# Attention scores as one float32 matmul for each of two heads, on the two halves of the array's rows

## What is computed

```python
t = tokens * rsqrt(mean(tokens * tokens, -1) + eps) * rms_w
gates = sigmoid(t @ w_gates)
q, k, v = (einsum('bnd,hde->bhne', t, w) for w in (wq, wk, wv))
score = where(causal_mask, -max, einsum('bhie,bhje->bhij', q, k) * scale)
attn = softmax(score, axis=-1)
out = einsum('bhij,bhje->bhie', attn, v) * gates
pred_values = einsum('bhne,hed->bnd', out, wo)
x = layernorm(x + pred_values)
x = layernorm(x + moe(x))      # 16 experts, top 2, and a shared expert
```

## Time and profile before

| | |
|---|---|
| median of 3 runs (lowest, highest) | 684.72 us (682.33, 686.58) |
| profiled execution, first to last instruction | 723.0 us |
| TensorE matmuls busy | 627.0 us, 87% |
| VectorE busy | 485.0 us, 67% |
| ScalarE busy | 417.0 us, 58% |
| GpSimd busy | 116.4 us, 16% |
| start, until the first scores | 0 to 32.5 us |
| attention, four head pairs | 32.5 to about 510 us |
| experts and last norm | about 510 to 723 us |
| mean granted TensorE clock | 0.944 of full speed |

### The profile page before, as it was taken

One profiled execution on the slowest core, in us unless ns is written; L12 is line 12 of the kernel. 1 busy time (PEld: TensorE's weight loads), 2 busy tenths in 40 slices (PEclk: granted clock), 3 DMA queues, 4 the chain that ended last, 5 costly groups with the idle time before them and its releaser, 6 DMA issues.

```text
span 723.0 us, 14787 instructions
## 1 busy us (share of the span) xinstructions
PE 627.0 (87%) x5300; PEld 511.7 (71%) x5300; DVE 485.0 (67%) x1556; ACT 417.0 (58%) x909; POOL 116.4 (16%) x229
## 2 busy tenths in 40 slices
PE   4899999999999999999999999998766079999930
PEld 2688888778888868888886888887623047888830
DVE  4788776698776778876768887767771033665636
ACT  4876566786655687665668766565330012655636
POOL 2000000000000000000000000000327600677630
PEclk9999999999999999999999999999599579999975
DMA  6600000130000040000007920003821100222233
GB/s 152 140 2 1 2 1 3 44 75 1 3 1 1 2 105 14 1 2 2 1 2 166 127 2 2 1 2 124 227 16 52 51 23 11 74 79 78 64 98 105
DMA packets 56393, 33.57 MB, mean 46 GB/s; under 512 B 23809, under 2 KB 49665, under 8 KB 56321
## 3 DMA queue, kind: packets, MB, share of 16 engines
q1 hardware_dynamic: 53760, 27.37, 18.8%
q0 software_dynamic: 2560, 5.26, 2.2%
HBM read 14.75 MB, written 9.48 MB: 34 GB/s over the span
## 4 chain that ended last, share of the span: by engine, by line
PE 74%; DVE 12%; another core or an unknown queue 5%; ACT 3%; issue 2%; DMA 2%; SPq 1%; POOL 0%; DVEq 0%; ACTq 0%; POOLq 0%
PE ps_t L966 18%; PE ps_o L1079 18%; PE ps_s L1048 11%; PE ps_s L1050 9%; PE ps_s L1198 5%; PE ps_o L1089 4%; PE ps_o L1186 3%; DVE k_l L671 3%; DVE q_hl L671 2%; PE ps_s L1122 2%; PE ps_t L1133 1%; PE ps_s L974 1%; ACT k_h L500 1%; DMA act_s<-y_rows 1%
## 5 line engine op out<-in xcount | busy, mean ns | idle before, releaser
L966 PE MATMUL ps_t<-ident,probs 128*128 128x128 f32 x1104 | 173.4, 275 | 11.6 <-ACT probs L512 11.5
L966 PEld LDWEIGHTS ps_t<-ident,probs 128*128 128x128 f32 x1104 | 134.9, 141 | 48.5 <-issue 11.4
L543 ACT ACTIVATE probs<-probs,nmax 128x128 f32<-128x128 f32 (+15 forms) x128 | 153.6, 1200 | 21.1 <-DVE nmax L766 12.4
L775 DVE COPY probsT<-ps_t 128x512 f32<-128x512 f32 (+3 forms) x160 | 91.3, 570 | 101.4 <-PE ps_t L966 100.4
L554 ACT ACTIVATE probsT<-ps_t 128x512 f32<-128x512 f32 (+3 forms) x160 | 89.7, 561 | 98.5 <-PE ps_t L966 97.1
L1048 PE MATMUL ps_s<-k_h,q_hl 128*128 128x512 f32 (+3 forms) x320 | 142.3, 448 | 0.4 <-DMA k_l<-k_l 0.4
L1079 PE MATMUL ps_o<-probsT,v_sb 128*64 128x128 f32 x2176 | 140.0, 277 | 1.3 <-DVE x_acc L790 1.2
L1079 PEld LDWEIGHTS ps_o<-probsT,v_sb 128*64 128x64 f32 x2176 | 116.8, 137 | 19.6 <-issue 14.6
L761 DVE TENSOR_SCALAR_CACHE_REDUCE probs<-ps_s 128x512 f32<-128x512 f32 x192 | 128.4, 686 | 0.7
L1050 PE MATMUL ps_s<-k_l,q_hl 128*128 128x512 f32 (+3 forms) x320 | 117.0, 366 | 0.0
L429 POOL TENSOR_TENSOR rden<-rsum,gate 128x2 f32<-128x2 f32 x64 | 12.6, 197 | 403.9 <-ACT probs L543 392.6
(11 more groups left out here) (144 smaller groups left out, 738.8 us busy)
## 6 DMA issues: line engine op xcount, KB each, us to landing
k_h<-k_h SPq DMA_DIRECT2D x32, 128.0 KB, 2.4
k_l<-k_l SPq DMA_DIRECT2D x32, 128.0 KB, 2.3
w_all<-in_L_ffn_W SPq DMA_DIRECT2D x2, 2048.0 KB, 12.6
xg<-x_sorted SPq DMA_DIRECT2D x48, 64.5 KB
x_sorted<-zeros SPq DMA_DIRECT2D x12, 256.0 KB, 9.5
act_s<-y_rows SPq DMA_DIRECT2D x8, 256.0 KB, 5.4
x_acc<-in_L_attn_tokens SPq DMA_DIRECT2D x4, 256.0 KB, 3.8
out<-x_acc SPq DMA_DIRECT2D x4, 256.0 KB, 2.3
```

The lines of the kernel that those rows point to most:

```text
L543: nc.scalar.activation(probs[s % 2][h][:, 0:w], probs[s % 2][h][:, 0:w], ACT.Exp, bias=nmax[:, row], scale=-1.0, accum_out=rsum[:, row]).t ...
L775: nc.vector.tensor_copy(probsT[s % 2][h][:, c * BT:c * BT + w // P, :].rearrange("p n i -> p (n i)"), ps_t[1][:, 0:w]).then_inc(moved1, 1)
L966: return nc.tensor.transpose(dst, src, ident[:, :])
```

## The change

Scores are made of plain float32. The projected K and Q of a head pair stay as they come out of the projection, head 0 on rows 0 to 63 and head 1 on rows 64 to 127, in one tensor each (`k_t`, `q_t`). A score group of a head is one float32 matmul over its own 64 rows. The two heads of a chunk are queued one behind the other, each into its own bank. ScalarE copies a projection in one operation of 128 rows; VectorE's subtraction and the transfers between the halves are gone. A bank of a projection is free after ScalarE's copy (`high`), so `freed` counts score groups alone, numbered by `score_of`. The order of units changes: scores are listed chunk by chunk with both heads, and the places of scores and turns are rounded to pairs; `ACT_LAG` has two new values; the chunk minima have a second buffer. A tensor `early_w_all` keeps the room that the removed tensors had.

```diff
     PLACE = {"scores": -0.15, "turn": 1.0, "times_v": 0.77, "times_wo": 0.6, "project": 0.0}
-    ACT_LAG = {"scores": 0.1, "turn": -0.3, "times_v": -0.15, "project": -0.3}
+    ACT_LAG = {"scores": 0.0, "turn": -0.2, "times_v": -0.15, "project": -0.3}
     DVE_LAG = {"turn": -0.2, "times_v": -0.4, "times_wo": 0.2}
...
-                stages.append([("scores", s, h, c, w) for h in range(2) for c, w in chunks[s]])
+                stages.append([("scores", s, h, c, w) for c, w in chunks[s] for h in range(2)])
...
-                    place = s + (i + PLACE.get(x[0], 0.5)) / len(units) + lag.get(x[0], 0.0)
+                    i2 = i // 2 * 2 if x[0] in ("scores", "turn") else i
+                    place = s + (i2 + PLACE.get(x[0], 0.5)) / len(units) + lag.get(x[0], 0.0)
...
+    score_of = [numbered(units, ("scores",)) for units in PE_UNITS]
...
-        q_hl = [sb(f"q_hl{h}", [P, N], f32r, attn) for h in range(2)]
-        k_h = [sb(f"k_h{h}", [P, N], f32r, attn) for h in range(2)]
-        k_l = [sb(f"k_l{h}", [P, N], f32r, attn) for h in range(2)]
+        q_t = sb("q_t", [P, N], f32, attn)
+        k_t = sb("k_t", [P, N], f32, attn)
+        sb("early_w_all", [P, 4 * N], f32, attn)
...
-        cmin = sb("cmin", [P, 2, NC], f32, attn)
+        cmin = sb("cmin", [P, 2, 2, NC], f32, attn)
...
-            def k_across(unit, highs, frees):
-                c = unit[3]
-                cols = slice(c * BANK, (c + 1) * BANK)
-                for k_part, part_ready, count in ((k_h, high, highs + 1), (k_l, freed, frees + 1)):
-                    sp.wait_ge(part_ready, count)
-                    for h in range(2):
-                        rows, other = slice(h * DH, (h + 1) * DH), slice((1 - h) * DH, (2 - h) * DH)
-                        sp.dma_start(k_part[h][other, cols].bitcast(f32),
-                                     k_part[h][rows, cols].bitcast(f32)).then_inc(k_twice, 16)
-
-            for x in START:
-                if x[1] == K:
-                    k_across(x, start_high_of[x], start_fill_of[x] + ONE)
-            for p in range(PAIRS - 1):
-                for x in PE_UNITS[0]:
-                    if x[:2] == ("project", K):
-                        k_across(x, p * KQ_FILLS + (KQ_FILLS + high_of[x]),
-                                 p * FREED + (KQ_FILLS + fill_of[x] + ONE))
...
-            sp.wait_ge(freed, ONE + KQ_FILLS + (PAIRS - 1) * FREED + GROUPS)
+            sp.wait_ge(freed, ONE + PAIRS * GROUPS)
...
-                    for h in range(2):
-                        rows = slice(h * DH, (h + 1) * DH)
-                        ins = nc.scalar.activation((k_h, q_hl)[w][h][rows, c * BANK:(c + 1) * BANK],
-                                                   ps_s[n % RING][rows, :], ACT.Copy)
-                    ins.then_inc(high, 1)
+                    nc.scalar.activation((k_t, q_t)[w][:, c * BANK:(c + 1) * BANK],
+                                         ps_s[n % RING][:, :], ACT.Copy).then_inc(high, 1)
...
-                        act.wait_ge(freed, p * FREED + (KQ_FILLS + n + 1 + ONE))
+                        act.wait_ge(freed, p * GROUPS + (n + 1 + ONE))
...
-            def project(unit, n, highs):
-
-                _, w, _, c, _ = unit
-                if w != V:
-                    dve.wait_ge(high, highs + 1)
-                    cols = slice(c * BANK, (c + 1) * BANK)
-                    for h in range(2):
-                        rows = slice(h * DH, (h + 1) * DH)
-                        free = slice((1 - h) * DH, (2 - h) * DH)
-                        low = (k_l[h][rows, cols], q_hl[h][free, cols])[w]
-                        ins = nc.vector.tensor_tensor(low, ps_s[n % RING][rows, :],
-                                                      (k_h, q_hl)[w][h][rows, cols].bitcast(f32), ALU.subtract)
-                    ins.then_inc(freed, 1)
...
-                if i >= 2:
-                    for w in (K, Q):
-                        x = ("project", w, 0, i - 2, 0)
-                        project(x, start_fill_of[x], start_high_of[x])
...
-                    least = cmin[:, h, c:c + 1] if (s, h) in long_rows else nmax[:, row]
+                    least = cmin[:, s % 2, h, c:c + 1] if (s, h) in long_rows else nmax[:, row]
...
-                        dve.wait_ge(freed, p * FREED + (KQ_FILLS + n + 1 + ONE))
-                        nc.vector.tensor_reduce(nmax[:, row], cmin[:, h, 0:c + 1], X, ALU.min).then_inc(row_max, 1)
+                        dve.wait_ge(freed, p * GROUPS + (score_of[("scores", s, h, c, w)] + 1 + ONE))
+                        nc.vector.tensor_reduce(nmax[:, row], cmin[:, s % 2, h, 0:c + 1], X, ALU.min).then_inc(row_max, 1)
...
-                    pe.wait_ge(freed, ONE + n - RING + 1)
+                    pe.wait_ge(high, n - RING + 1)
...
+                filled = {n: x for x, n in fill_of.items()}
+
                 def free_bank(n):
 
                     if n < RING:
                         pe.wait_ge(v_ready, p * NC + (n + 1))
+                        return
+                    held = filled[n - RING]
+                    if held[0] == "scores":
+                        pe.wait_ge(freed, p * GROUPS + (ONE + score_of[held] + 1))
+                    elif held[1] == V:
+                        pe.wait_ge(v_ready, (p + 1) * NC + (NC - held[3]))
                     else:
-                        pe.wait_ge(freed, p * FREED + (ONE + KQ_FILLS + n - RING + 1))
+                        pe.wait_ge(high, (p + 1) * KQ_FILLS + (high_of[held] + 1))
 
                 def scores(s, h, c, w, n):
                     t = ORDER[s]
-                    if s == 0 and h == 0:
-
-                        pe.wait_ge(freed, p * FREED + (ONE + KQ_FILLS))
-
-                        pe.wait_ge(k_twice, p * (64 * NC) + 64 * NC)
+                    if s == 0 and h == 0 and c == 0:
+
+                        pe.wait_ge(high, (p + 1) * KQ_FILLS)
                     free_bank(n)
-                    q = q_hl[h][:, t * P:(t + 1) * P]
-                    nc.tensor.matmul(ps_s[n % RING][:, 0:w], q, k_h[h][:, c * BANK:c * BANK + w],
-                                     start=True, stop=False)
-                    nc.tensor.matmul(ps_s[n % RING][:, 0:w], q, k_l[h][:, c * BANK:c * BANK + w],
-                                     start=False, stop=True).then_inc(fill, 1)
+                    rows = slice(h * DH, (h + 1) * DH)
+                    nc.tensor.matmul(ps_s[n % RING][:, 0:w], q_t[rows, t * P:(t + 1) * P], k_t[rows, c * BANK:c * BANK + w],
+                                     start=True, stop=True).then_inc(fill, 1)
```

More of the change, by code:

```diff
@@ L55, in attention_moe_layer @@
     KQ_FILLS = PROJECTIONS - NC
-    FREED = FILLS - NC
     RING = 4
@@ L126, in attention_moe_layer @@
     start_fill_of = numbered(START, ("project",))
+    score_of = [numbered(units, ("scores",)) for units in PE_UNITS]
     high_of = {x: n for n, x in enumerate(x for x in PE_UNITS[0] if x[0] == "project" and x[1] != V)}
-    start_high_of = {x: n for n, x in enumerate(x for x in START if x[1] != V)}
     def started(*unit):
@@ L133, in attention_moe_layer @@
     assert len(fill_of) == FILLS and FILLS % RING == 0 and PROJECTIONS % RING == 0
-    assert all(x[:2] == ("project", V) for x, n in fill_of.items() if n >= FREED)
+    assert all(x[:2] == ("project", V) for x, n in fill_of.items() if n >= FILLS - NC)
     ctx = ExitStack()
@@ L267, in attention_moe_layer @@
         z_ready, ez_ready, gate_ready = sem("z_ready"), sem("ez_ready"), sem("gate_ready")
-        pair_w, pair_wo, k_twice, v_ready = (sem(n) for n in ("pair_w", "pair_wo", "k_twice", "v_ready"))
+        pair_w, pair_wo, v_ready = (sem(n) for n in ("pair_w", "pair_wo", "v_ready"))
         fill, freed, high = sem("fill"), sem("freed"), sem("high")
@@ L533, in norm, with pair @@
                     nc.scalar.activation(rows[:, 1, cols, 0:D], rows[:, 0, cols, 0:D], ACT.Copy).then_inc(rows_ready, 1)
-            def pair(p, units, fill_of):
+            def pair(p, units, fill_of, score_of):
                 def exps(s, h, n):
@@ L570, in pair @@
                     elif stage == "scores" and (c, w) == chunks[s][-1]:
-                        exps(s, h, fill_of[x])
+                        exps(s, h, score_of[x])
                     elif stage == "turn":
@@ L579, in _ @@
             for p in range(PAIRS - 1):
-                pair(p, ACT_UNITS[0], fill_of)
-            pair(PAIRS - 1, ACT_UNITS[1], last_fill_of)
+                pair(p, ACT_UNITS[0], fill_of, score_of[0])
+            pair(PAIRS - 1, ACT_UNITS[1], last_fill_of, score_of[1])
             norm("stats", n3)
@@ L795, in pair @@
                     stage, s, h, c, w = x
-                    if stage == "project":
-                        project(x, fill_of[x], p * KQ_FILLS + (KQ_FILLS + high_of.get(x, 0)))
-                    elif stage == "scores":
+                    if stage == "scores":
                         scores(s, h, c, w, fill_of[x])
@@ L810, in _ @@
             for p in range(PAIRS - 1):
```

(8 more changed lines are left out.)

## The result

The changed kernel takes 765.69 us, the median of three runs (763.74 to 767.88), against 684.72: a ratio of 1.118 (95% interval 1.113 to 1.123), +81 us.

What follows compares the result with a forecast made beforehand. The prediction took TensorE's stream to bound the attention part; 15 (stream) + 54 (queue waits) - 6 (pair ends) - 4 (start) = +59 us on the profiled 723.0, scaled to +56, 741 us; range 689 to 785.

Steps and rivals of the forecast that it cites:

- rival (c): Score matmuls: the two heads overlap only by half, 1.29 us a pair of 512, +90 us, 770 us; chance 0.12.
- Queue waits: Attention stages: in the new order TensorE waits for exponentials and ScalarE's moves, 13.6 us a head pair, +54 us.
- Stage index 8: Stage turning tile index 8 (2048 keys): TensorE waits 1.3 us for the first turn, 1.2 for the third turn group.
- TensorE's stream: TensorE in attention: float32 score pairs and changes between whole and split array, net +3.8 us a head pair, +15 us.
- 21 groups: Score groups behind a value product in the kernel before: counted as 1.0 us a head pair on TensorE.
- The overlap of the heads: Score matmuls: heads on rows 0 to 63 and 64 to 127 run side by side, 0.86 us for both.
- (d): Score matmuls: no overlap of the heads at all, +131 us, 809 us; chance 0.06.
- Pair ends: Three head-pair ends: VectorE's subtractions go and one of ScalarE's two copies, -6 us in all, bounds -3 and -8.
- start: Kernel start: the wait for a scaling behind the subtractions and the half-array copies of K go, -4 us, bounds -1 and -6.
- Rival (a): Attention: changes to and from a row split cost nothing and queues have slack, -26 us, 660 us; chance 0.12.
- (b): Attention: row split priced as for columns, but no waits, +5 us, 689 us; chance 0.08.
- The scaling: Whole kernel: profiled execution 5.6% longer than the runs' median, so +59 us was scaled to +56.

Runs made afterwards that it cites:

- e5: The changed kernel itself, unaltered, timed again against the kernel before: ratio 1.113 (1.109 to 1.117), 808.0 against 726.2 us.
- e3: Changed kernel with each head's score matmul over all 128 rows, so the array is not split for scores: ratio 1.152 to the kernel before.
- e7: Changed kernel with VectorE's order alone altered, scores ahead of the copies of turned probabilities: ratio 1.081 to the kernel before.
- e1: Kernel before with its split scores kept, only the changed kernel's unit order, lags and second minima buffer taken: 802.6 against 726.6 us, ratio 1.105.

## Why the prediction was right, and where its sizes were off

The forecast was slower by 56 us, with the new order as the larger part; it is slower by 81. The sign, the mechanism and the place held; two terms of the sum were short and one was missing. The time alone would not have shown that: 766 lies above the forecast's own 735 to 750 and next to rival (c)'s 770, and it is the trace that decides between them. In the second head pair of after, which is 142.96 us long:

- **Queue waits**, forecast 13.6 us a head pair: measured 16.3, starts of the turn groups against their usual distance to the operation before. Stage index 8, walked chunk by chunk, has 1.5 + 1.0 = 2.4 us (forecast 1.3 + 1.2); the list behind it was close too: index 2 1.0, 3 0.7, 5 1.7, 6 1.6, 7 1.8, 9 1.8, 10 1.2, 11 0.4, and 2.1 at the last (forecast 1.7). Missed were index 4 (1.0) and 12 (0.4), put down as "about none". For four pairs 65 us instead of 54.
- **TensorE's stream**, forecast +3.8 us a head pair: measured +6.1 (125.0 without waits and without the clock's drop below, against 118.9 before). The score pair itself was right: 1.15 us from turn to turn, the turn's own 0.11 left out, against 1.16 forecast from the value product's rows, and 0.94 before for both heads. One step of the working was low by itself: 21 groups at the 0.03 us that its rows show (0.34 for 0.31) are 0.6 us, not 1.0, which takes 0.4 off the stream of before. What it lacked is the slower slot of the turn behind a pair (0.165 for 0.109); 29 pairs stand directly before turns, which makes 1.6 of the missing 2.3 us. The other 0.3 was not assigned.
- **The overlap of the heads**, on which everything hung: complete. Rival (c), half an overlap, would need the first records 0.43 apart, and (d), none, 0.86; they are 0.007 apart. The prediction took (c) from the strict program order of matmuls in the Trainium skill, "TensorE: Matmul & The Clock Gate", The mechanism. That was read too narrowly: by the same section matmuls on different tiles of the array overlap, each starting about 4 ns behind the one before, and only their order is kept. The trace agrees with that, with 7 ns, and the section speaks against (c). The rule of the Trainium skill, "TensorEngine Tiling (Array Packing)", Key Properties, is that changing the tiling mode drains TensorE. The trace agrees for rows: 0.20 us instead of 0.11 where a pair meets a turn.
- **Pair ends**, -2 us each, and **start**, -4: measured -1.8 (16.2 to 14.4; the waits go, and nothing is late in their place) and -4.6. The start came out partly by luck: about 1.5 of the 4.6 are the clock of before, which was not in the working, and e5, the same kernel, gains only 1.9.
- **Rival (a)**, free changes and slack in the queues, falls on both counts; (b), a split price with no waits, falls on the waits.
- **The scaling** from 59 to 56 was a wrong step, though a small one: the 38 us by which the profiled execution exceeded the median were not 5.6% on every stage, but one wait in the experts' part. The difference carries over unscaled (83 and 81).
- **TensorE's clock** was not in the sum at all. An estimate of its cost is half of each stretch of 3.4 us at 0.50, about 1.7 us in each of three head pairs, below.

Sum of the terms as measured in the second head pair: 4 x (6.1 + 16.3) + 3 x 1.7 - 3 x 1.8 - 4.6 = 85 us, against 83.1 between the two traces.

## What to carry to other kernels

When work of two streams is put side by side on one engine, their results come due together: walk what the other engines then have queued between two operations that this engine needs, because here the order alone cost 76 of the 82 us, and the float32 matmuls on top of it 6; with the waits mended they cost 2.7 to 3.9 us a head pair. Change the order alone first, on the old arithmetic; it is one edit, and it separates the two. A split of the array between operations on the whole array costs at each meeting, here 0.15 to 0.2 us in and out, so it pays only for groups that are long against that, as here (e3, without the split, is 29 us slower); and when a profiled execution is longer than the runs, look for a stage that holds the surplus before scaling a difference.

## What the runs showed that was not expected

**TensorE's clock falls after the longest wait.** Its timeline, and windows with the granted clock in the third column from the end:

```profile
289.92 0.85 PE L922 MATMUL ps_t<-ident,probs 128*128 128x128 f32 x6 [1.91 <-ACT probsT L532]
290.70 3.63 PE L1039 MATMUL ps_o<-probsT,v_sb 128*64 128x128 f32 x32
```

```profile
286.00:290.00 4.00, 2.09 (x15) 1.24 (x12) 1.72 (x6) 2.41 (x7) 0.19 (x1) 1.00 0.01 2
290.00:292.00 2.00, 2.00 (x18) 1.83 (x20) 1.04 (x3) 0.60 (x1) 0.00 (x0) 0.69 0.00 0
292.00:294.00 2.00, 2.00 (x23) 1.96 (x20) 0.00 (x0) 0.00 (x0) 0.00 (x0) 0.50 0.00 0
294.00:297.00 3.00, 3.00 (x32) 2.29 (x30) 1.65 (x7) 1.95 (x7) 0.20 (x1) 0.97 0.00 0
```

After 1.9 us of idleness six turns run at their usual pace, and then the granted clock is 0.50, which is 1.2 GHz, for about 3.4 us: the value product's 32 records hold the array for 3.6 us where others of that size take 1.9. The place is the turn of index 13, where TensorE waits longest. It happens there in three of four head pairs of after, three of four of e5 and all four of e7, the kernels with the wait of 1.9 us; in e5's second pair the same wait of 1.91 us left the clock at 1.00. No value product of 32 records was slow in before or in any of the other experiments, whose longest waits inside a head pair are 1.8 us (e1) and less. Something like it stands at the start of before: a wait of 1.79 us, then 0.50 for 3.4 us from 21.15. So a wait there can cost nearly twice its length. What decides between 0.50 and 1.00 after the same wait stays open.

**The price of a split by rows** shows at three places: 0.20 for 0.11 us on the way in, 0.53 for 0.43 in the first slot, and 0.52 for 0.43 in the last, with 0.165 for 0.109 in the first turn behind it. A split by columns costs 0.09 on the way in and 0.15 within.

**The wait of some 35 us in the experts' part** is in the profile of before and in those of all eleven experiments, and not in that of after, which is e5's kernel. Nothing tried here bears on its cause, and it stays open.
